# Residual, norms, quantisation and ternary products placed group by group inside the last slot-attention turn and between the first attention's maxima

## What is computed

```python
x = x + tanh(g_xattn[0]) * slot_attention(layernorm(x), ctx)   # 3 turns: attention over 154 context rows, then a GRU cell
x = x + tanh(g_ffn[0]) * ternary(layernorm(x))                 # round each token to int8, multiply with a matrix of -1, 0, 1
x = x + tanh(g_xattn[1]) * mha1(layernorm(x), ctx, ctx)        # 16 heads of 16, 154 keys
x = x + tanh(g_ffn[1]) * tanh(((h @ w) @ a1) @ a2 + bias)      # h = layernorm(x)
x = x + tanh(g_xattn[2]) * mha2(layernorm(x), ctx)             # as mha1
# behind it: a mixture of 8 experts, a fourth attention, a mixture of 32 experts
```

## Time and profile before

| | us |
|---|---|
| three runs | 1490.34, 1504.26, 1516.75 |
| median | 1504.26 |
| the profiled execution | 1502.2 |
| its span in the trace | 1500.4 |
| PE, DVE, ACT, POOL busy in it | 1267.0, 721.5, 437.0, 285.5 |

### The profile page before, as it was taken

The page is one execution under the profiler, slowest core; times in us unless marked ns, Lnnn a source line. Parts: engine busy times, 40 slices in busy tenths (PEclk is TensorE's granted clock), DMA queues, the critical chain, the costliest instruction groups (busy, mean ns, idle before and its releaser), DMA issues.

```text
span 1500.4 us, 19335 instructions
## 1 busy us (share of the span) xinstructions
PE 1267.0 (84%) x6360; PEld 774.8 (52%) x6361; DVE 721.5 (48%) x2083; ACT 437.0 (29%) x833; POOL 285.5 (19%) x306
## 2 busy tenths in 40 slices
PE   5999999999347799999998758999678797899983
PEld 3534434434234244444443548999555455777762
DVE  7363563463974245565464540111266652455446
ACT  2222222222052235454443302333233210233320
POOL 2111111000122000000000040111112662355550
PEclk9999999999677689999996868999866799999996
DMA  9999994000010000000000374555309223345436
GB/s 313 339 336 332 328 335 146 0 0 0 19 39 1 0 1 1 1 1 1 31 1 1 117 238 152 176 183 189 110 27 352 85 88 91 116 147 150 145 123 259
DMA packets 140424, 186.75 MB, mean 124 GB/s; under 512 B 8672, under 2 KB 124896, under 8 KB 140224
## 3 DMA queue, kind: packets, MB, share of 16 engines
q1 hardware_dynamic: 130800, 159.28, 34.2%
q0 software_dynamic: 9552, 26.52, 4.8%
HBM read 83.71 MB, written 102.06 MB: 124 GB/s over the span
## 4 chain that ended last, share of the span: by engine, by line
PE 61%; DVE 14%; issue 6%; DMA 5%; POOL 5%; SPq 4%; ACT 4%; another core or an unknown queue 0%; DVEq 0%; POOLq 0%; ACTq 0%
PE psum L1886 13%; PE psum L1214 6%; PE psum L2078 6%; PE psum L1225 5%; POOL xs L872 3%; PE psum L2134 3%; DMA xs<-xn,arena 3%; DVE arena L2677 2%; PE psum L2111 2%; PE psum L1879 2%; PE psum L2064 2%; PE psum L2158 2%; SPq L957 2%; PE psum L1914 2%; SPq L958 2%
## 5 line engine op out<-in xcount | busy, mean ns | idle before, releaser
L1886 PE MATMUL psum<-arena 128*128 128x512 f32 x432 | 205.8, 628 | 0.0
L2677 DVE TENSOR_REDUCE arena<-psum 128x4 f32<-128x616 f32 x128 | 102.2, 798 | 128.8 <-PE psum L2078 127.5
L1886 PEld LDWEIGHTS psum<-arena 128*128 128x128 f32 x432 | 83.6, 200 | 120.4 <-issue 119.6
L2078 PE MATMUL psum<-arena 32*128 32x308 f32 x512 | 114.0, 525 | 24.2 <-DVE arena L2677 22.9
L1142 POOL DMA_INDIRECT ys<-xnT,arena x96 | 92.4, 962 | 114.2 <-DVE xnT L1108 92.0
L2252 ACT ACTIVATE arena<-psum,arena 128x512 f32<-128x512 f32 x72 | 49.1, 686 | 173.5 <-PE psum L1886 161.0
L2370 ACT ACTIVATE arena<-psum 128x2048 f32<-128x2048 f32 x40 | 75.0, 1875 | 79.2 <-PE psum L2115 60.6
L1785 POOL TENSOR_TENSOR x_tok<-x_tok,add_row 128x1024 f32<-128x1024 f32 x16 | 37.7, 2365 | 293.4 <-ACT xn L1688 163.8
L1002 PE MATMUL psum<-arena,xn 128*128 x384 | 89.9, 388 | 1.4 <-ACT xn L1053 0.9
L2078 PEld LDWEIGHTS psum<-arena 32*128 32x128 f32 x512 | 42.6, 203 | 93.2 <-DVE arena L2677 61.9
L1214 PEld LDWEIGHTS psum<-side,arena 128*128 128x128 f32 x736 | 87.4, 195 | 2.7 <-ACT side L1259 1.6
(11 more groups left out here) (397 smaller groups left out, 2111.5 us busy)
## 6 DMA issues: line engine op xcount, KB each, us to landing
xs<-zeros SPq DMA_DIRECT2D x8, 8576.0 KB, 59.7
arena<-in_W SPq DMA_DIRECT2D x31, 1024.0 KB, 11.9
xn<-xs SPq DMA_DIRECT2D x96, 134.0 KB
arena<-in_gate_up SPq DMA_DIRECT2D x4, 2048.0 KB, 16.2
arena<-ys SPq DMA_DIRECT2D x4, 2048.0 KB, 14.6
arena<-in_down SPq DMA_DIRECT2D x4, 1024.0 KB, 15.5
xs<-zeros SPq DMA_DIRECT2D x1, 2990.0 KB, 16.8
side<-xs SPq DMA_DIRECT2D x23, 130.0 KB
```

The lines of the kernel that those rows point to most:

```text
L1886: ins = pe.matmul(bank[dict(hn=4, r=5, z=6, xn=7)[k]][:], lhs[:, cols], r, start=(start and n == 0), stop=(stop and n == len(w) - 1))
L2078: ins = pe.matmul(bank[4 + i][:, 0:2 * M].rearrange("p (h m) -> p h m", h=2), qhT[rows, n % 3, c, t * P:(t + 1) * P], keys[rows, l, c, b, ...
L2677: dve.tensor_reduce(neg[:, n % 2, t, 2 * pair:2 * pair + 2, 2 * c:2 * c + 2], psum[:, 4:6, 0:2 * M].rearrange("p b (h m) -> p b h m", h=2) ...
```

## The change

- **Slot turn.** In the last turn, for q = 1 to 3, PE gets the slot transposes of group q - 1 (`finish_slots_tensor`), the transposes of quantised groups 0 and 1 (`tern_turn_tensor`) and the ternary product of group 0 (`tern_product_tensor`). DVE gets residual, norm and quantisation of groups 0 and 1 and the ternary residual and next norm of group 0. ACT applies three norms and copies two turned groups.
- **Norms.** The norms of stages 1 and 2 go the way of `ln_ready`: ACT applies them.
- **Front.** `flow()` starts with ternary product 1, turn, the last slot residuals, two of seven context products, query, and the norms of groups 2 and 3.
- **Maxima.** The rest (quantise 2 and 3; ternary 1, 2, 3; their norms; the other five context products of the first attention; turn and query of group 1) stands between the 16 `most`. DVE takes it in portions of eight pieces after each `most` (`advance_early`: a heavy piece counts 2, the last one of a quantisation 4, its reduction 6).
- **Second attention.** Its seven context products move out of that stretch, as `second` operations, three in each of slots 0 and 1 and one in slot 2.
- **Start.** `tri_fold_tensor` (now two sums of two halves in bank 7, two copies) moves to before the turns of groups 2 and 3; unpacking of the ternary weights moves ahead of the slot turns.
- **Constants and loads.** The attention's constant tiles are filled by 41 POOL instructions behind POOL's last work in the slot turns and ahead of all its bias rows. The arena is laid out anew, so that SP can load the first attention's weights after `context_copied("vw", 4)` and the second's after `ms_ready`.

```diff
--- before.py
+++ after.py
...
 
-            yield from (("turn", 0, 0), ("turn", 0, 1), ("query", 0, 0), ("query", 0, 1))
-            between = iter((("context", 1, 0), ("turn", 1, 0), ("turn", 1, 1), ("context", 1, 1), ("query", 1, 0),
-                            ("query", 1, 1)))
+            yield from (("product", 1), ("turn", 0, 0), ("turn", 0, 1), ("finish", 3), ("context", 0), ("query", 0, 0),
+                        ("query", 0, 1), ("norm1", 2), ("norm1", 3))
+            after = {3: (("norm2", 1),), 4: (("context", 1),), 5: (("tern_turn", 2), ("turn", 1, 0)),
+                     6: (("product", 2), ("turn", 1, 1)), 7: (("context", 2),), 8: (("tern_turn", 3), ("query", 1, 0)),
+                     9: (("product", 3), ("query", 1, 1)), 11: (("norm2", 2),), 14: (("norm2", 3),)}
             for k in range(16):
                 yield ("most", 0, k)
-                if k % 2:
-                    yield from itertools.islice(between, 1)
+                yield from after.get(k, ())
             yield ("shift", 0)
+            second = iter([("second", k) for k in range(7)])
             for n in range(SLOTS):
...
             yield from most()
             yield from settle("settle", settled)
+            yield from itertools.islice(second, 1)
             yield ("weigh", n, 0)
             yield from most()
             yield from behind("project", n - 1, 0)
             yield from most()
             yield from behind("project", n - 1, 1)
             yield from most()
...
             turn(last_turn)
 
+        def mha_constants_gpsimd(pool):
...
+            pool.memset(neg_bf.rearrange("p t (j q) -> p (t j) q", j=4)[:, :, 12:], 0.0).then_inc(ctx_made, 1)
+            pool.memset(ctxR.rearrange("p c b (q m) -> p (c b q) m", q=4)[:, :, MR:], 0.0)
+            for c in range(C):
+                for b in range(B):
+                    ins = pool.tensor_copy(ctxR[:, c, b].rearrange("p (q m) -> p q m", q=4)[:, :, 0:MR],
+                                           ctxT[:, c, b * M + P:(b + 1) * M].unsqueeze(1).broadcast_to([P, 4, MR]))
+            ins.then_inc(ctx_made, 1)
+            pool.wait_ge(wmha_loaded[0], 6 * 16)
+            for l in range(2):
+                for c in range(C):
+                    for h in range(2):
+                        pool.tensor_tensor(kbias[:, l, c, h:h + 1], vmha[:, l, 1, c:c + 1], mask16[:, h:h + 1], ALU.mult)
...
+            add_row_gpsimd(pool, 2, 1, 1)
             shift_parts_gpsimd(pool, 0)
+            add_row_gpsimd(pool, 2, 1, 2)
+            add_row_gpsimd(pool, 2, 1, 3)
+            shift_parts_gpsimd(pool, 1)
+            shift_parts_gpsimd(pool, 2)
             mha_rows_gpsimd(pool, 1)
             pool.wait_ge(*cvec_ready.at(1, 1))
-            for n in range(1, SLOTS):
+            for n in range(3, SLOTS):
                 if 0 <= n - (G - 1) < G:
                     add_row_gpsimd(pool, 4, 2, n - (G - 1))
...
                 ins.then_inc(context_summed.sem, 1)
+            tri_fold_tensor(pe)
...
                     recurrent_part(q, 0)
+                    if it is last_turn and q == 3:
+                        tern_product_tensor(pe, 0)
                     input_part(q, 0)
+                    if it is last_turn:
+                        finish_slots_tensor(pe, q - 1)
                     recurrent_part(q, 1)
                     if it is not last_turn:
                         for _ in square_sums(it + 1, q - 1):
                             pass
+                    elif q >= 2:
+                        tern_turn_tensor(pe, q - 2)
                     input_part(q, 1)
...
+        def finish_slots_tensor(pe, q):
+
+            pe.wait_ge(h_ready, 8 * ITERS + 2 * q + 2)
+            if q:
+                pe.wait_ge(*x_done.at(0, q))
+            else:
+                pe.wait_ge(attn_ready, ITERS * G)
...
+        def tern_turn_tensor(pe, g):
+
+            pe.wait_ge(xq_ready, g + 1)
+            if g:
+                pe.wait_ge(*x_done.at(1, g))
+            else:
+                pe.wait_ge(consts_made, 3)
+            for c in range(C):
...
+        def tern_product_tensor(pe, g):
+
+            if g == 0:
+                pe.wait_ge(tern_ready, 4)
+            pe.wait_ge(*xnT_ready.at(1, g + 1))
...
+        def context_product(pe, l, k, dst):
+
+            if k < 2:
...
+        first_context = ((4, 5), (0, 1), (0, 1, 0))
...
+                pe.wait_ge(wmha_loaded[0], 6 * 16)
+                pe.wait_ge(h_ready, 8 * ITERS + 8)
+            elif part == 1:
+                pe.wait_ge(*x_done.at(0, G))
             else:
                 pe.wait_ge(ctx_made, 3)
...
+                act.wait_ge(tri_folded, k + 1)
+                act.activation(wtri12[:, k].rearrange("p c n -> p (c n)"), bank[7][:], ACT.Copy).then_inc(tri_copied, 1)
             for g in range(GB, G):
...
+                    if it is last_turn:
+                        if q < 3:
+                            normalise_scalar(act, 1, q - 1)
+                        else:
+                            normalise_scalar(act, 2, 0)
+                        if q >= 2:
+                            tern_scalar(act, q - 2)
...
-                    act.wait_ge(*project_ready.at(1, g - 1))
+        def tern_scalar(act, g):
+
+            act.wait_ge(*turned.at(1, g + 1))
+            if g >= 2:
+                act.wait_ge(*project_ready.at(1, g - 1))
+            act.activation(qT[:, g % 2].rearrange("p c n -> p (c n)"), bank[2].bitcast(BF16), ACT.Copy).then_inc(xnT_ready.sem, 1)
...
                     argument(q, 0)
+                    if it is last_turn:
+                        if q < 3:
+                            finish_slots_vector(dve, main, q - 1)
+                            run(next_norm_parts(dve, main, 0, q - 1))
+                        else:
+                            run(ternary_parts(dve, main, 0))
                     argument(q, 1)
                     new_slots(q, 0)
                     new_slots(q, 1)
+                    if it is last_turn and q < 3:
+                        run(quantise(dve, main, q - 1))
                 ch.close()
 
             with dve.Fori(0, ITERS - 1) as it:
...
             for t in range(GT):
                 ch.step(dve.tensor_scalar(xn[:, g, t, 0:D], xn[:, g, t, 0:D], scale[:, t:t + 1], ROUND, ALU.mult, ALU.add))
+                yield True
...
+                while early and pieces > 0:
+                    first = next(iter(early))
+                    cost = next(early[first], early)
+                    if cost is early:
+                        early.pop(first)
+                    else:
+                        pieces -= 2 if cost is True else cost or 1
 
             def filled(op):
...
+                    finish_slots_vector(dve, ch, 2)
+                    norm2 = next_norm_parts(dve, ch, 0, 2)
+                    run(itertools.islice(norm2, GT + 1))
+                    finish_slots_vector(dve, ch, 3)
+                    together(norm2, next_norm_parts(dve, ch, 0, 3))
+                elif op[0] == "norm1":
+                    early["quantise", op[1]] = quantise(dve, ch, op[1])
+                elif op[0] == "tern_turn":
+                    finish_early(("quantise", op[1]))
+                elif op[0] == "norm2":
+                    finish_early(("tern", op[1]))
             finish(5)
...
+                sp.wait_ge(*context_copied.at("vw", 4))
                 for l in range(2):
+                    sp.dma_start(vmha[:, l], d[f"vec{l + 1}"].rearrange("p (v c) -> p v c", c=C)).then_inc(wmha_loaded[0], 16)
+                for l in range(2):
+                    if l:
+                        sp.wait_ge(ms_ready, ITERS * G)
                     for k, name in enumerate(("wq", "wk", "wv", "wo")):
-                        sp.dma_start(wmha[:, l, k], weight(d[f"{name}{l + 1}"])).then_inc(wmha_loaded[l], 16)
-                    sp.dma_start(vmha[:, l], d[f"vec{l + 1}"].rearrange("p (v c) -> p v c", c=C)).then_inc(wmha_loaded[l], 16)
+                        sp.dma_start(wmha[l][:, k], weight(d[f"{name}{l + 1}"])).then_inc(wmha_loaded[l], 16)
             if last_stage >= 5:
                 sp.wait_ge(*x_done.at(3, G))
...
```

408 lines of the change are left out of this document (187 added, 221 removed).

## The result

The changed kernel takes 1451.89 us (median of four runs, 1443.17 to 1464.40) beside 1504.72 of the kernel before on the same chip: a ratio of 0.9669, 95% interval [0.9621, 0.9717]. Its profiled execution took 1443.17 us (span 1441.4) and is the shortest of its four, so the two traces differ by 59.0 us and not by 52.8. In this document medians are of all runs, while ratios and intervals leave out slow runs, those over 1.5% above the fastest of their kernel: five of the ten of `b_warm`, two of the seven of `a_fold_slot0`, one of the four of `a_warm`.

The account below looks back on a forecast made before the run. PE was 61% of the span, but the 82.35 us between last product and first maximum were mostly DVE's chain. The steps, 5.3 + 5.2 - 64.7 + 17.9 + 8.5 = -27.8 us, gave 1475 us, range 1458 to 1492.

Parts of the forecast that it names:

- Step 1, start: Before the turns of groups 2 and 3: the weight fold moved there is hidden by nothing, +5.3 us, bounds 3.8 and 8.
- Step 2, last turn: In the last slot turn PE is full, so each insertion counts: +5.2 us, with DVE's work hidden; at worst 10.
- The rival of a stalled turn: In the last turn insertions wait for DVE or ACT, +5 us, and PE's clock drops for a part: 1482; chance 0.08.
- Step 3, gap: From the last product of the turns to the first maximum: 82.35 us becomes 17.7, a step of -64.7 us.
- the 2.8 us for a low clock: Between last product and first maximum: 2.8 us added because PE's clock is low at first after idle time.
- Step 4, maxima: The first attention's 16 maxima, with DVE's moved work among them: 38.1 us becomes 56, +17.9, bounds 46 and 70.
- the nine light cycles: Maxima 0 to 3 and 10 to 14, where PE has nothing else: 22.4 us together.
- the six heavy ones: Maxima cycles 4 to 9, which carry PE's other work: 30 us, between 22.4 at the high clock and about 38 at the low.
- POOL's extra 2 us: In the maxima: POOL's bias rows now fall among DVE's tiny steps, for which 2 us were added.
- Step 5, slots 0 to 2: Seven context products go where PE is full: +8.5 us, 7.1 at the high clock and 1.4 for slot 0's; bounds 5 and 13.
- Slot 0's clock far from 0.65: A sign that the prediction is wrong: slot 0's mean granted clock is not near the 0.65 it had before.
- the clock comes back: Rival: high clock through maxima cycles 4 to 9 (22.4 for 30) and part of slot 0 (4 us): another 12 off, 1463; chance 0.19.

Follow-up runs that it names:

- b_warm: The kernel before with dummy products of 256 columns on PE, two behind each of maxima 11 to 15 and six behind the 16th: 1499.03 us, ratio 0.9911.
- a_fold_slot0: The changed kernel with the weight fold taken from the start and put into slot 0: 1440.82 us, ratio 0.9644 to the kernel before.
- a_warm: The changed kernel with dummy products of 256 columns on PE behind maxima 11 to 16: 1456.01 us, ratio 0.9711 to the kernel before.
- the bare maxima: The changed kernel with all norms, quantisations, ternary products and context products ahead of the first maximum: 1471.05 us, ratio 0.9847 to the kernel before.
- the split: The changed kernel with the weight fold's first half behind the turns' last product, its second behind the 12th maximum: 1438.68 us, ratio 0.9625 to the kernel before.
- the fold alone: The kernel before with only the two halves of the weight fold moved to the start: 1494.77 us, ratio 1.0038.
- the late constants: The changed kernel with 100 further memsets in POOL's constants ahead of the attention: 1498.25 us in one execution.

## Where the prediction held and where it failed

- **Step 1, start.** Right: +5.7 and +6.4 for +5.3, and 1 to 11 us when done alone.
- **Step 2, last turn.** Right: +4.5 for +5.2, with no wait of PE from the first insertion to the last product. DVE carries 67.76 us there and is on time. The rival of a stalled turn is dead.
- **Step 3, gap.** 15.0 for 17.7. The wait for the new slots is 4.48 us (5.0), the last wait 0.78 (0.7). The term that was too big is the 2.8 us for a low clock: PE is busy 9.73 us for the 9.2 at the high clock. The transposes at 3.41 stood behind similar idle time, but here the clock was granted at 0.89. What the taken-away work was worth was the part sized best. Two experiments say where it went: 34 us of the gap come back when the last turn's insertions stand behind it, 26 when the maxima are bare. The earlier weight loads and the constants on POOL were not taken back alone; their part isn't shown.
- **Step 4, maxima.** 50.7 for 56. Of the sum's parts, the nine light cycles took 19.9 for 22.4, the six heavy ones 28.5 for 30, the end 2.3 for 1.7, and POOL's extra 2 us isn't to be seen: its rows at 395.53 and 422.45 held up none of DVE's tiny steps. A light cycle costs 2.3 us at the low clock whether DVE has other work in it or not, as the bare maxima show; I had let DVE's pieces lengthen it.
- **Step 5, slots 0 to 2.** +0.7 for +8.5 in the first traces, +2.5 in the means, and this is the step that failed. The products' own price was right. At clock 1.00 slot 1 takes 38.26 us without them (kernel before, third trace) and 41.72 with three (`a_warm`): 3.5, where 3 to 4 were said. At 0.75 slot 0 takes 40.74 without and 46.87 with three: 6.1. What failed is that I kept slot 0's clock at 0.65, the value of before. It was 0.87 in all four traces, and by the dummies the distance from 0.65 to 1.00 is worth 9.8 us. "Slot 0's clock far from 0.65" was named as a sign of being wrong, and "the clock comes back" as a rival with 4 us in slot 0; I gave it 0.19 because PE is less busy per maximum. Half of that rival came: its other half, cycles 4 to 9 at the high clock in 22.4 us, did not, since they took 28.5 and the maxima's clock is 0.69. PE is less busy there (35.06 of 50.67 us, before 28.77 of 38.12), and the slot's clock rose all the same, so a stretch's busy share alone doesn't foretell it.
- **Slot 3 to the end.** Not in the sum, -4.5 in the mean. Some 2.6 of it repeats in slots 3 to 6 (179.3 us in all four traces of the changed kernel, 182.2 in three of before, 181.2 in the one with the better clock).
- **Executions.** The two first traces differ by 10.2 us in the first turns, 3.9 in the means. I had scaled by 2.1 us for an execution's luck. Whether a part belongs to the change is open. In all seventeen traces of this document, the ten with the fold at the start have the first two turns at 218.9 us in the mean (213.5 to 223.6) and the seven without it there at 222.9 (217.0 to 225.4), with the same instructions. That would give back most of what the fold costs at the start, and fits the split, whose 6.5 us don't show in the time; the fold alone, at 5.7 us more in time, speaks against it.

Together: 0.7 + 2.7 + 5.4 + 7.8 us from steps 2 to 5, 4.9 behind slot 2 and 10.2 in the turns, less the 0.4 that step 1 was short, are the 31.2 between -27.8 and -59.0, within rounding. By the means, in which the luck of a single execution weighs less, the two largest misses are step 4 (6.2) and step 5 (6.0). Step 3's 2.8 us and step 5's 0.65 are of one kind, a low clock carried over from rows of the kernel before. Step 4's miss is spread over the light cycles (2.5), the heavy ones (1.5) and POOL's term (2.0). What stays open is why the changed kernel's slot 0 gets 0.87 every time when behind the late constants, with the same maxima, it gets 0.78; only that the clock sets its length, and that PE's work just before can set the clock, is shown.

## What to carry to other kernels

Price a product that is added to a full stage at the clock the stage will have, not at the one it had: measure the same stage at two clocks in repeated traces, and make the clock's return a term of the sum. A serial chain on one engine is cheapest under another engine's dense stretch: here the insertions cost PE 4.5 us and kept 34 off the gap. Read one stage in several executions before a difference of two traces is given a cause.

## What was not expected of the hardware

Sixteen dummy products in waits of PE cost 0.65 us and took 9.8 off the stage behind them in the kernel before; in the changed one they took nothing off the maxima and the two slots behind them (135.1 us for 135.7), and its time is no better.

A DVE instruction with two SBUF inputs (SBUF is the on-chip memory that the engines share) stood until a bias row of POOL had ended. After, POOL's row and DVE's step beside it, which takes 0.69 us otherwise:

```profile
342.77 2.71 POOL L1846 TENSOR_TENSOR x_tok<-x_tok,add_row 128x1024 f32<-128x1024 f32 x1 [35.47 <-ACT xn L1713]
```

```profile
343.31 2.72 DVE L2574 SCALAR_TENSOR_TENSOR arena<-arena 128x512 f32<-128x512 f32 x1
```

This is what the Trainium skill, "SBUF — State Buffer", section "Who interferes with whom", says of such pairs, and the trace agrees. It happened twice in the last turn and cost nothing, since no PE wait followed. The 41 constants were over after 9 us, the longest of them 0.96, a memset, which reads nothing:

```profile
306.35 0.96 POOL L1787 MEMSET arena<- 128x1024 f32 x1
```

In the bare maxima the same thing did cost: two steps of a norm, 0.16 us each otherwise, took 2.19 and 2.26 beside two bias rows, and PE's second `most` stood behind them.

```profile
428.92 4.64 POOL L1845 TENSOR_TENSOR x_tok<-x_tok,add_row 128x1024 f32<-128x1024 f32 x2
```

```profile
429.09 2.19 DVE L1644 SCALAR_TENSOR_TENSOR nwt<-nwt 128x4 f32<-128x4 f32 x1
431.31 2.26 DVE L1669 SCALAR_TENSOR_TENSOR shift_ln<-meanvar,nwt 128x4 f32<-128x4 f32 x1
```
